# A chunked recurrence with its mix: the chunk loop written out, another table set for the roots, gelu's table load named, h1 and h2 two matmuls to a slot

## The reference

```
x = layernorm(x + L0_attn(x))   # state-space recurrence, 512 channels x 128 states, over 512 steps
x = layernorm(x + L0_ffn(x))    # silu(x W1) * (x W2), then gelu(. H1), gelu(. H2), then . W3
x = layernorm(x + L1_attn(x))   # q, k, v; cumulative sums of exp(k) and exp(k) v; swiglu; out projection
x = layernorm(x + L1_ffn(x))    # 8 experts, the best 2 of each row

# the recurrence of L0_attn, for every step t:
h = exp(dt_t * A) * h + (dt_t * B_t) * u_t ;  y_t = h . C_t
# y is then divided by its root mean square, times norm_w, times silu(z), and projected
# gelu is the exact one (with erf); the norms take 1/sqrt(var + eps)
```

## Time and profile before

| | |
|---|---|
| median of three runs | 5777.41 us |
| profiled execution | 5808.26 us |
| its span | 5806.4 us |
| granted clock, mean | 0.862 |
| PE busy | 4852.6 us (84%) |
| DVE busy | 3830.3 us (66%) |
| ACT busy | 3417.0 us (59%) |
| POOL busy | 3980.6 us (69%) |

### The profile page before, as it was taken

How to read it: one execution, slowest core, us unless ns; L and a number is a source line. 1 busy time by engine, 2 the same in 40 slices (tenths; PEclk the granted TensorE clock), 3 DMA queues, 4 the chain that set the end, 5 groups by cost and what they waited for, 6 DMA issues and landing times. The chain is left out here.

```text
span 5806.4 us, 82633 instructions
## 1 busy us (share of the span) xinstructions
PE 4852.6 (84%) x20772; PEld 1699.4 (29%) x20772; DVE 3830.3 (66%) x4276; ACT 3417.0 (59%) x3983; POOL 3980.6 (69%) x2256
## 2 busy tenths in 40 slices
PE   5449998998999889889979998998899785399991
PEld 3211112222222222222222222222222344266661
DVE  7848888777887788788878887887888403000003
ACT  4536666777677767777777767777767512111111
POOL 2359998998899789889979897998889200400004
PEclk7755558998999899899989998998999895699995
DMA  2357766776667566666756775666677221333322
GB/s 89 94 172 254 240 233 222 253 255 221 242 236 265 202 234 245 230 223 235 260 214 232 247 254 199 251 242 241 228 235 261 81 76 41 113 117 109 108 101 94
DMA packets 313082, 1139.77 MB, mean 196 GB/s; under 512 B 69664, under 2 KB 123424, under 8 KB 306720
## 3 DMA queue, kind: packets, MB, share of 16 engines
q1 hardware_dynamic: 298688, 1065.24, 52.5%
q0 software_dynamic: 13920, 69.22, 3.6%
HBM read 1077.17 MB, written 69.73 MB: 198 GB/s over the span
## 5 line engine op out<-in xcount | busy, mean ns | idle before, releaser
L1542 POOL TENSOR_TENSOR s_h<-s_decay,s_h 128x768 f32<-128x768 f32 x2048 | 3703.9, 1842 | 444.9 <-ACT s_decay L1197 407.1
L1580 DVE TENSOR_TENSOR s_h<-s_h,bank 128x1024 f32<-128x1024 f32 x2048 | 2473.0, 1216 | 531.6 <-PE bank L803 305.0
L1197 ACT ACTIVATE s_decay<-s_decay,s_a_neg 128x1536 f32<-128x1536 f32 x1024 | 1605.5, 1568 | 246.9 <-DMA s_decay<-dt_rows 245.7
L829 PE MATMUL bank<-s_h,s_cdiag 128*32 128x512 f32 x8192 | 1275.6, 699 | 4.2 <-ACT s_y L1209 4.2
L1202 ACT ACTIVATE bank<-bank,s_a_neg 128x512 f32<-128x512 f32 x1024 | 672.4, 657 | 743.5 <-PE bank L817 740.7
L803 PE MATMUL bank<-s_vrow,s_brow 9*128 9x512 bf16 x4096 | 845.1, 425 | 208.9 <-DVE s_h L1580 167.2
L1570 DVE TENSOR_TENSOR s_h<-bank,s_h 128x512 f32<-128x512 f32 x1024 | 699.2, 683 | 2.8 <-ACT bank L1202 2.7
L927 PE MATMUL bank<-m_ma,m_w 128*128 128x512 f32 x1024 | 579.4, 659 | 44.7 <-ACT m_mb L1273 39.3
L803 PEld LDWEIGHTS bank<-s_vrow,s_brow 9*128 9x128 bf16 x4096 | 203.3, 92 | 1407.0 <-issue 1403.7
L941 PE MATMUL bank<-m_mb,m_w 128*128 128x512 f32 x1024 | 581.0, 660 | 30.9 <-ACT m_ma L1278 17.5
L817 PE MATMUL bank<-s_drow,s_unit 3*128 3x512 bf16 x1024 | 436.9, 427 | 74.2 <-DMA s_drow<-dt_parts 49.2
(11 more groups left out here) (195 smaller groups left out, 4201.1 us busy)
## 6 DMA issues: line engine op xcount, KB each, us to landing
s_decay<-dt_rows SPq DMA_DIRECT2D x1024, 768.0 KB, 5.1
m_w<-in_units SPq DMA_DIRECT2D x210, 512.0 KB, 5.3
s_vrow<-v_parts SPq DMA_DIRECT2D x1024, 36.0 KB
s_brow<-b_parts SPq DMA_DIRECT2D x1024, 9.0 KB
v_parts<-p_part SPq DMA_DIRECT2D x24, 512.0 KB, 3.0
slots<-in_x_tiles SPq DMA_DIRECT2D x128, 96.0 KB, 5.2
e_xs<-slots SPq DMA_DIRECT2D x24, 512.0 KB
expert_out<-e_made SPq DMA_DIRECT2D x23, 512.0 KB, 9.2
```

Source lines behind the costliest of these rows:

```text
L829: mm = pe.matmul(bank[q * 32:(q + 1) * 32, Y0], cdiag[:, hf * LANES + q, at * BLK:(at + 1) * BLK], h[:, t % 2, hf * LANES + q], start=(at ...
L1197: act.activation(decay[:, k % RING], decay[:, k % RING], ACT.Exp, scale=a_neg[:, 1:2]).then_inc(decay_ok, 1)
L1542: pool.tensor_tensor(h[:, t % 2, g * PAIR:(g + 1) * PAIR, DCOLS:], decay[:, k % RING, g % 2 * PAIR:(g % 2 + 1) * PAIR], h[:, (t + 1) % 2, ...
L1580: dve.tensor_tensor(h[:, t % 2, g * PAIR:(g + 1) * PAIR], h[:, t % 2, g * PAIR:(g + 1) * PAIR], bank[:, X0 + n % 2 * PAIR:X0 + (n % 2 + 1) ...
```

## The change

Five things are done, all in `stream_phase`:

- the loops over chunks of SP, PE, ACT, POOL and DVE become Python loops: the program has every chunk written out, with constants in its waits and addresses;
- `root` asks for the table set named natural_log_exp_and_others ahead of its Ln;
- `gelu_1` and `gelu_2` ask for the set named gelu_and_others ahead of their wait for the product;
- each h1 and h2 product takes four slots, two matmuls in each (`share`), instead of eight slots with one;
- other slots and half steps for some pieces of the mix. For h1 the last slots were 82, 92, 101, 109, 119, 127, 136, 145 and are 82, 91, 100, 108, 118, 126, 135, 144.

```diff
-GT_AT = (21, 22, 23, 25)
+GT_AT = (21, 22, 23, 24)
...
-UP_AT = (46, 50, 54, 58, 62, 66, 70, 74)
-H1_AT = ((75, 76, 77, 78, 79, 80, 81, 82), (85, 86, 87, 88, 89, 90, 91, 92), (94, 95, 96, 97, 98, 99, 100, 101),
...
-H2_AT = ((147, 148, 149, 150, 151, 152, 153, 154), (156, 157, 158, 159, 160, 161, 162, 163), (165, 166, 167, 168,
...
+UP_AT = (46, 50, 54, 58, 63, 66, 71, 74)
+H1_AT = ((76, 78, 80, 82), (85, 87, 89, 91), (94, 96, 98, 100), (102, 104, 106, 108), (112, 114, 116, 118), (120,
+    122, 124, 126), (129, 131, 133, 135), (138, 140, 142, 144))
+H2_AT = ((147, 149, 151, 153), (156, 158, 160, 162), (165, 167, 169, 171), (178, 180, 182, 184), (190, 192, 194,
+    196), (204, 206, 208, 210), (214, 216, 218, 220), (224, 226, 228, 230))
...
-SILU_SWI_AT = (181, 185)
+SILU_SWI_AT = (180, 183)
...
-CW_AT = (81, 87)
-CKV_AT = (93, 101)
-SEED_AT = 20
-KEEP_AT = (53, 64)
-DEN_AT = (116, 123)
-REC_AT = (120, 129)
-DIV_AT = (147, 153)
+CW_AT = (80, 87)
+CKV_AT = (99, 108)
+SEED_AT = 19
+KEEP_AT = (54, 68)
+DEN_AT = (114, 124)
+REC_AT = (121, 131)
+DIV_AT = (141, 149)
 STATS_2_AT = (206, 207)
-NORM_1_AT = {1: (0, 1, 2, 3)}
+NORM_1_AT = {2: (0, 1, 2, 3)}
 X_SQ_AT = {2: (0, 1, 2, 3)}
-TO_UNIT_AT = {3: (0, 1, 2, 3)}
-Y_SQ_AT = {2: (0, 1), 3: (2, 3)}
+TO_UNIT_AT = {2: (0,), 3: (1, 2, 3)}
+Y_SQ_AT = {0: (0,), 1: (1,), 2: (2, 3)}
...
+def share(slots, n, count):
+    at, per = slots.index(n), count // len(slots)
+    return range(at * per, (at + 1) * per)
...
-                        weights(m + 1, FULL[i], (m, names[i - WRING]))
+                        weights(m + 1, (TAIL if m + 1 == CHUNKS - 1 else FULL)[i], (m, names[i - WRING]))
...
-                        hidden_1(m, j, (H1_AT[j].index(n),), False)
+                        hidden_1(m, j, share(H1_AT[j], n, KH), False)
...
-            with pe.Fori(2, CHUNKS - 1) as c:
+            for c in range(2, CHUNKS - 1):
                 body(c, c - 1, False)
...
             def root(m, mean, dst, eps, ln_sem, ok_sem):
+                act.preload_act_table_set("natural_log_exp_and_others")
                 act.activation(dst, mean, ACT.Ln, bias=eps).then_inc(ln_sem, 1)
...
             def gelu_1(m, j, tail):
+                act.preload_act_table_set("gelu_and_others")
                 act.wait_ge(S("h1_ps"), FIRST + m * KH + j + 1)
...
-            with pool.Fori(0, CHUNKS) as c:
+            for c in range(CHUNKS):
```

More of the change, by code:

```diff
@@ L426 @@
 GATE_AT = (44, 48, 52, 56, 60, 64, 68, 72)
-UP_AT = (46, 50, 54, 58, 62, 66, 70, 74)
-H1_AT = ((75, 76, 77, 78, 79, 80, 81, 82), (85, 86, 87, 88, 89, 90, 91, 92), (94, 95, 96, 97, 98, 99, 100, 101),
-    (102, 103, 104, 105, 106, 107, 108, 109), (112, 113, 114, 115, 116, 117, 118, 119), (120, 121, 122, 123, 124,
-    125, 126, 127), (129, 130, 131, 132, 133, 134, 135, 136), (138, 139, 140, 141, 142, 143, 144, 145))
-H2_AT = ((147, 148, 149, 150, 151, 152, 153, 154), (156, 157, 158, 159, 160, 161, 162, 163), (165, 166, 167, 168,
-    169, 170, 171, 172), (178, 179, 180, 181, 182, 183, 184, 185), (190, 191, 192, 193, 194, 195, 196, 197), (204,
-    205, 206, 207, 208, 209, 210, 211), (214, 215, 216, 217, 218, 219, 220, 221), (224, 225, 226, 227, 228, 229,
-    230, 231))
+UP_AT = (46, 50, 54, 58, 63, 66, 71, 74)
[3 more added lines that the diff above has]
+    196), (204, 206, 208, 210), (214, 216, 218, 220), (224, 226, 228, 230))
 SWI_AT = (174, 176, 188, 189)
@@ L768, in _ @@
             body(1, 0, False)
-            with sp.Fori(2, CHUNKS - 1) as c:
+            for c in range(2, CHUNKS - 1):
                 body(c, c - 1, False)
@@ L1090, in mix @@
                     if n in H2_AT[j]:
-                        hidden_2(m, j, (H2_AT[j].index(n),), False)
+                        hidden_2(m, j, share(H2_AT[j], n, KH), False)
                 for pair in range(2):
@@ L1444, in _ @@
             body(1, 0, False)
-            with act.Fori(2, CHUNKS - 1) as c:
+            for c in range(2, CHUNKS - 1):
                 body(c, c - 1, False)
@@ L1753, in _ @@
             body(1, 0, False)
-            with dve.Fori(2, CHUNKS - 1) as c:
+            for c in range(2, CHUNKS - 1):
                 body(c, c - 1, False)
```

## The result

| | before | after |
|---|---|---|
| median | 5775.49 us (4 runs) | 5621.37 us (4 runs, 5619.35 to 5631.0) |
| profiled span | 5806.4 us | 5620.9 us |
| granted clock, mean | 0.862 | 0.871 |
| POOL idle until ACT has a decay | 407.1 us | 256.0 us |

The ratio is 0.9731, 95% interval [0.9712, 0.9749]: 154 us less.

A forecast was written before the change was run, and what follows sets the result against it. The prediction took waits that reach POOL, mostly for ACT's decay, to bound the kernel. Loops (50 us) and roots (24) made 74, the rest 0: 5777.4 - 74 = 5703 us, with 5685 to 5725 given 0.45 and a range from 5640 to 5762.

The forecast's parts named there:

- Floor and ledger: POOL's products: a chunk's floor is 455.4 us, and the change is worth what it takes off POOL's 444.9 us idle.
- Loops, -50: Chunk loops written out: 46.5 us in chunks 3 to 6 plus 3.5; four jump stalls, 18 us, the least.
- Roots, 48 halved to -24: One table set for Ln and Exp: 7.7 us in six chunks, 2 in chunk 1; half counted, 24 us.
- the third rival's case: Roots' table loads: asked loads always made, 9 instead of 7, 15 us at most, 5710 to 5718; no separate chance.
- the root of q and k: Its loads and the last copy for transposed y, moved to slot 24: up to 6.3 us together, taken as -4.
- Gelu's ask, 0: Gelu's table load already stands ahead of the wait, so asking is worth 0; up to 15 loads added in the tail.
- Pairs, 0: h1 and h2, two matmuls to a slot: PE's work the same, from -1.1 to +1.1 us per product, taken as 0.
- other slots, 0: Moved ACT passes and DVE scans, reciprocals and divisions: 0, from -2 to +2 us in a chunk.
- The burst that turns the sign: Rival: two matmuls ahead of e_rows and gelu delay the decay 1.12 us at 112 products, +125 us; 5860, chance 0.08.
- Only the jumps: Rival: table-load savings lost in PE and DMA waits, written-out chunks give 18 to 46 us; about 5745, chance 0.22.
- All of it holds: Rival: loops 50 and roots 48 both in full, 5679, down to 5640 with Tanh served and better overlap; chance 0.17.
- The signs named: Expected traces: no PE issue wait over 2 us at chunk starts, chunks 3 to 6 near chunk 2, seven loads, others.

The follow-up runs named there:

- e5: The kernel before with the five loops over chunks written out and nothing else changed: 5709.36 us, ratio 0.9892 to the kernel before.
- e10: The kernel before with SP's loop alone written out, the other engines keeping theirs: 5723.23 us, ratio 0.9895 to the kernel before.
- e16: The kernel before with all loops written out and the roots asking for the common table set: 5672.26 us, ratio 0.9811 to the kernel before.
- e14: The kernel before with all loops written out and h1 and h2 two matmuls to a slot: 5712.48 us, ratio 0.9876 to the kernel before.
- e4: The changed kernel with all pieces of the mix other than h1 and h2 back in their old slots: 5663.17 us, ratio 0.9802 to the kernel before.
- e15: The kernel before with all loops written out and the mix's pieces other than h1 and h2 at the new slots: 5719.64 us, ratio 0.9889.
- e2: The changed kernel with h1 and h2 back at one matmul to a slot in the old slots: 5678.71 us, ratio 0.9826 to the kernel before.
- e3: The changed kernel with the roots not asking for the common set of Ln and Exp: 5664.94 us, ratio 0.9808 to the kernel before.
- e17: The changed kernel with gelu_1 and gelu_2 not asking for their table set: 5620.69 us, ratio 0.9710 to the kernel before.
- e11: The kernel before with SP's loop written out and h1 and h2 two matmuls to a slot: 5731.97 us, ratio 0.9909 to the kernel before.
- e6: The kernel before with h1 and h2 two matmuls to a slot in the new slots, loops kept: 5771.53 us, ratio 0.9981 (10 runs).

## Why the prediction was wrong

**Floor and ledger: right.** POOL's idle time was what could be won; 156.3 of its 444.9 us went, 151.1 of them waits for ACT's decay.

**Loops, -50: right in size** (e5: 62, from 42 to 83 by its interval), too narrow in cause. The jump stalls were taken for the least of it and SP's program for a check at the side. e10 turns this round: SP alone gives 1.05%, 61 us.

**Roots, 48 halved to -24: right for the chunks, and the tail was left out.** The roots' asks give 36 to 47 us by the ratios, in four companies (e5 to e16, e14 to e4, e15 to e2, e3 to the change), near the 48. Chunks 2 to 7 of the profiled executions give 15 to 27 us of it, 21.6 in the mean, which is what the halved term says. The premise that asked loads of a loaded set are not made was wrong (nine loads, not seven, the third rival's case, priced at 7 to 15 us more). At the first root, costed at -0.7, nothing came: DVE's operation there ends at the same time in e5. At the root of q and k PE has no wait left ahead of the projection, against the earlier trace rows, but the roots win there (slots 32 to 47) 16 to 18 us with the copy behind the root and 0 to 4 with the copy in front: the slot of the copy does it by itself. The term that was left out is the tail. Ten roots stand there one behind the other. Groups of ACT behind POOL's last product, before and then after:

```profile
L1213 ACT ACT_TABLE_LOAD x10 | 12.8, 1283 | 0.2
L1215 ACT ACT_TABLE_LOAD x10 | 12.8, 1283 | 0.2
```

```profile
L1216 ACT ACT_TABLE_LOAD x10 | 12.8, 1283 | 36.1 <-DVE m_mv L1596 35.9
```

That is 12.8 us less; the time behind POOL's last product falls by 13.4 us (mean of the four kernels of the table with the asks, 1243.1, against the four without, 1256.5). Together 21.6 + 13.4 = 35 us; the 1 to 12 us that are left to the 36 to 47 lie in chunk 1 and in the spread of the runs.

**Gelu's ask, 0: right** (e17).

**Pairs, 0, and other slots, 0: the step that failed.** "PE's work is the same" doesn't hold: 123 us of PE are gone, and the gelu waits with them. The sum took each edit by itself. Together they give 46 us, and apart nothing; the slots' own gain (the copy, -4 a chunk in the roots' account) was there, and the loss that it meets is the arrears of PE that the pairs take away (DVE's waits for PE in slots 80 to 143: 88 us in e15, 38 in e3). Of the 80 us between forecast and result, 46 are this block, 23 the roots (13 of them the tail) and 12 the loops.

**The rivals.** The burst that turns the sign, 5860: refuted; the stretch of h1 is shorter with pairs in every company (80 to 143 in the table). Only the jumps, 5745: refuted. "All of it holds", 5679 down to 5640, came nearest and was given 0.17; even its lower end was too high, since it counted the pairs at 0: their bound of 112 x 1.1 = 123 us was worked out for both sides and used on the slow side only.

**The signs named:** no issue stall (right), chunks 3 to 6 within 5 us of chunk 2 (wrong for chunk 4, which has 12 us more and two holds), PE's 3.87 us gone (right), seven loads (nine), slots behind 75 unchanged (wrong: 80 to 255 take 2029.4 us where they took 2082.8).

**A mechanism not foreseen** worked against the change: POOL's products hold DVE's scans at the new slots (two to six in each kernel that has them there, one at most at the old ones). silu_swi is held only in kernels with the pairs, at the new slots and at the old ones (six times in e4, four in e11, three in e6), so the pairs have a part in it.

## What to carry over

When several engines hand one wait round, an edit measured alone can show nothing and the same edit in company 50 us: bound the pair of edits, not each, and keep a bound that was worked out inside the range. Count what an edit does in the parts that run alone (the tail), where nothing hides it. Where one queue issues all transfers, set its time for a step beside the floor's: 4.50 against 3.56 us here. Before a shorter wait is credited to an edit, look at when the operation behind it ends. Where POOL streams through SBUF, a DVE operation with two SBUF operands can cost some 5 us with each issue, and the stretch behind it pays again at PE's lower clock.

## What the runs showed of the hardware

- Two float32 matmuls of 128x512 that follow each other take 1.98 us, one alone 1.12, at 2.4 GHz.
- DVE operations of 512 columns with both operands in SBUF took 4.9 to 7.0 us in some chunks beside POOL's products, and at most 2.9 us in the others. All six of the changed kernel ended 0.5 to 1.1 us after a run of POOL's products. DVE's reciprocal (one operand) took 3.29 to 3.35 us every time.
- This loop cost its time through the queue that issues DMAs: 61 us of 5785 for SP's loop alone, with 4.50 us to a group of issues against 3.49. PE's stalls at the jumps were 4.2 to 5.0 us each, and those of 4.4 and 4.5 us that e10 still shows cost nothing that can be told.
- A table set asked for by name was loaded even where it was in: 48 loads for the 48 roots of the changed kernel.
